# Three loads and one store change places in the DMA order of SyncE, in a fused attention and feed-forward kernel

## The reference

```python
xn = _layernorm(x, axis=-1)
# attention: 16 heads of 16 features
qkv = xn @ w_qkv.T + b_qkv
att = einsum('bhqd,bhkd->bhqk', q, k) / sqrt(16) + bias      # bias depends on (i - j) and the head
att = softmax(where(causal, att, -inf))
attn = einsum('bhqk,bhkd->bhqd', att, v) -> [B, T, C] @ w_proj.T + b_proj
# feed-forward: x and kernel rounded to float8 (e4m3), multiplied in float32, scaled back
return x + attn + ffn
```

## Time and profile before

| what | value |
|---|---|
| time, median of 3 runs | 825.46 us (824.64 to 831.89) |
| time of the profiled execution | 820.26 us |
| its span on the core | 818.5 us |
| granted TensorE clock, mean | 0.973 of full speed |
| PE busy | 747.2 us (91%) |
| DVE busy | 628.9 us (77%) |
| ACT busy | 581.0 us (71%) |
| POOL busy | 528.2 us (65%) |
| queue q1 | 102.96 MB, 60.4% of 16 engines |

### The profile page before, as it was taken

How to read it: one execution, slowest core, us unless ns; L and a number is a source line. 1 busy time by engine, 2 the same in 40 slices (tenths; PEclk the granted TensorE clock), 3 DMA queues, 4 the chain that set the end, 5 groups by cost and what they waited for, 6 DMA issues and landing times.

```text
span 818.5 us, 23154 instructions
## 1 busy us (share of the span) xinstructions
PE 747.2 (91%) x6313; PEld 510.0 (62%) x6313; DVE 628.9 (77%) x2395; ACT 581.0 (71%) x1258; POOL 528.2 (65%) x525
## 2 busy tenths in 40 slices
PE   6869999999999999999999999999999999999883
PEld 3546666666676667657676666657666666767552
DVE  3767878887977878788788878787787879778722
ACT  4236767777786877778687777778677777867671
POOL 6433568567666867667676757766685776667580
PEclk8859999999999999999999999999999999999998
DMA  6834666567566656666566657756665775666502
GB/s 170 165 68 95 114 145 123 129 148 144 127 138 153 118 130 138 138 145 137 141 121 151 123 127 162 142 126 137 148 117 123 155 143 124 139 130 121 120 24 86
DMA packets 55548, 106.07 MB, mean 130 GB/s; under 512 B 10464, under 2 KB 30432, under 8 KB 55520
## 3 DMA queue, kind: packets, MB, share of 16 engines
q1 hardware_dynamic: 53192, 102.96, 60.4%
q10 hardware_dynamic: 2328, 2.77, 1.0%
HBM read 18.68 MB, written 8.91 MB: 34 GB/s over the span
## 4 chain that ended last, share of the span: by engine, by line
PE 49%; ACT 15%; SPq 11%; issue 9%; DMA 7%; DVE 5%; ACTq 3%; DVEq 1%; POOL 0%; POOLq 0%
SPq L328 11%; PE misc_a L539 8%; PE misc_a L655 8%; PE scoreT_b L629 6%; PE misc_b L539 6%; ACT probs L911 6%; PE scoreT_a L629 3%; DMA stacks<-neg_max_T 3%; PE misc_b L655 3%; PE score_a L606 3%; PE score_c L606 2%; ACT qk_parts L818 2%; ACT out_T L884 2%; ACT attn_hi L893 2%; ACT xnT_hi L807 1%
## 5 line engine op out<-in xcount | busy, mean ns | idle before, releaser
L1187 POOL TENSOR_SCALAR_AFFINE_SELECT probs<-probs 128x512 f32<-128x512 f32 x256 | 159.5, 635 | 244.7 <-ACT probs L911 242.8
L989 DVE CUSTOM_DVE_ANT_0 score_b<-score_b,causal_mask_q 128x384 f32<-128x384 f32 (+3 forms) x321 | 161.9, 521 | 119.6 <-PE score_b L606 118.4
L989 DVE CUSTOM_DVE_ANT_0 score_a<-score_a,causal_mask_q 128x512 f32<-128x512 f32 x319 | 173.1, 559 | 8.1 <-PE score_a L606 4.1
L911 ACT ACTIVATE probs<-scoreT_b 128x384 f32<-128x384 f32 (+1 forms) x256 | 134.5, 525 | 60.7 <-issue 23.7
L989 DVE CUSTOM_DVE_ANT_0 score_c<-score_c,causal_mask_q 128x256 f32<-128x256 f32 (+3 forms) x384 | 171.4, 474 | 2.3 <-PE score_c L606 2.2
L911 ACT ACTIVATE probs<-scoreT_a 128x512 f32<-128x512 f32 (+1 forms) x256 | 145.6, 569 | 14.0 <-PE scoreT_a L632 7.4
L989 DVE DVE_READ_ACCUMULATOR2_ANT row_max<- 128x1 f32 x1024 | 142.9, 140 | 0.0
L911 ACT ACTIVATE probs<-scoreT_c 128x384 f32<-128x384 f32 (+1 forms) x256 | 136.2, 532 | 3.7 <-PE scoreT_c L632 3.3
L655 PE MATMUL misc_a<-probs,v_ones 128*32 128x128 f32 (+3 forms) x1536 | 131.2, 438 | 0.4 <-POOL probs L1187 0.4
L629 PE MATMUL scoreT_a<-stacks 64*128 64x512 f32 (+3 forms) x320 | 108.3, 358 | 21.8 <-DMA stacks<-neg_max_T 13.8
L629 PE MATMUL scoreT_b<-stacks 64*128 64x384 f32 (+3 forms) x320 | 119.5, 393 | 7.6 <-ACT probs L911 7.1
(11 more groups left out here) (241 smaller groups left out, 1948.9 us busy)
## 6 DMA issues: line engine op xcount, KB each, us to landing
stacks<-qk_parts SPq DMA_DIRECT2D x128, 512.0 KB, 8.1
x_ring<-in_L_attn_x SPq DMA_DIRECT2D x16, 512.0 KB, 3.6
xn<-recips SPq DMA_DIRECT2D x31, 256.0 KB
out<-x_ring SPq DMA_DIRECT2D x15, 512.0 KB, 3.0
attn<-out_T SPq DMA_DIRECT2D x48, 128.0 KB, 2.6
stacks<-neg_max_T SPq DMA_DIRECT2D x128, 4.0 KB
attn<-out_T ACTq DMA_DIRECT2D x16, 128.0 KB, 2.9
low_features<-neg_max_T SPq DMA_DIRECT2D x124, 4.0 KB
```

The lines of the kernel that those rows point to most:

```text
L911: A(probs_slot(g, k), STB[(SLOTS * g + k) % 3][:, 0:w], ACT.Exp).then_inc(exp_done, 1)
L989: last = V.tensor_tensor_reduce(bank, bank, CMQ[:, T - w:T], 1.0, LEAST, ALU.add, ALU.max, MX[:, g % 2, 8 * h + 4 + qt:8 * h + 5 + qt])
L1187: last = GP.affine_select(out=d, in_=d, compare_op=ALU.is_ge, fill=0.0, base=0, pattern=[[0, HU], [1, P]], channel_multiplier=-1)
```

## The change

SyncE's list of one batch is reordered. Before, the inverses' store came first, then x's load, the spread, and the next batch's first stack. Now x's load comes first, then the store, the stack, and the spread. No instruction of another engine moves, and nothing is added or taken away.

```diff
@@ -462,20 +462,20 @@
                     sp.wait_ge(st_ready, ROW * b)
                 load_stack(b, 3)
                 load_max(b, 1)
-                if not first:
-                    store_recips(b - 1)
                 if load:
                     if not first:
                         sp.wait_ge(out_stored, 16 * b)
                     sp.wait_ge(x_loaded, 16 * (b + 2))
                     load_x(b + 2)
                 if not first:
-                    spread_recips(b - 1, last)
+                    store_recips(b - 1)
 
                 if not last:
                     wait_alone(sp, (w_loaded, 16), (st_ready, ROW * b + SLOTS),
                                (ql_ready, 4 * (b + 1) + 2))
                     load_stack(b + 1, 0)
+                if not first:
+                    spread_recips(b - 1, last)
                 load_max(b, 2)
                 regroup(b, 0, first)
```

## The result

| kernel | median | runs | mean clock of the profiled run |
|---|---|---|---|
| before | 827.25 us | 4 (824.64 to 831.89) | 0.973 |
| changed | 875.64 us | 4 (871.65 to 886.7) | 0.933 |

The medians are of all four runs; the ratio, 1.056 with a 95% interval of 1.049 to 1.064, leaves out the run of 886.7 us, which fell into the slower of two states that executions of one kernel show. The forecast was 815 us, in a range of 811 to 828; it failed in sign and in size. The span of the profiled execution went from 818.5 to 872.5 us, 54 us more.

What follows compares the result with a forecast made beforehand. PE was taken as bound by its waits for the maxima, 13.8 us in all; 0.8 us off each gave 10.4 us, `divide`'s delay counted as nothing. Off the 825.46 us median that made 815 us, range 811 to 828.

Steps and rivals of the forecast that it cites:

- What bounds the kernel: PE is busy 91%; its largest wait is for the row maxima at unit (2,0), 13.8 us in 15 waits.
- A batch gets shorter by nearly what this wait loses: PE at (2,0): batch length less the wait for the maxima is constant within 0.4 us.
- x's load forward: SyncE: x's load issued once the second maxima are out, near 439 in batch 8; its 0.42 us issue costs nothing.
- The stack's earlier start: SyncE: the stack starts at 444.72 in place of 445.89 in batch 8, 1.17 us earlier.
- The spread moves behind the stack. Its issues end near 447.6, ...: SyncE, batch 8: the spread's issues end near 447.6, so the maxima are issued at most 0.3 us later.
- whole weight: DMA engines: the spread's full transfer time, estimated at 1.6 us, added between the stack and the maxima.
- best: Maxima in batch 8: the spread behind the stack costs nothing, their issue ends at 452.47 in place of 454.26, 1.8 us earlier.
- worst of this kind: Maxima in batch 8: the spread adds 1.6 us, their issue ends at 454.07, 0.2 us earlier.
- `divide`'s delay: POOL, batch 8: the spread lands at 454.3, so `divide` is 1.0 us late, costed at nothing.
- The slack of 1.5 us: POOL, batch 8: `divide` may start as late as 454.78 instead of 453.30 for nothing.
- The one on the slow side: POOL and DVE: a late spread makes `divide` the bound, 6 to 12 us slower, about 834; chance 0.15.
- The first rival: SyncE's DMAs: same bytes ahead of the maxima, 0.2 us a batch left, 822 us, no tellable change; chance 0.30.

Runs made afterwards that it cites:

- e5: Kernel before with a wait added on SyncE, so the third maxima are issued near 454.5 of batch 8 in place of 447.5; 886.01 us, ratio 1.076.
- e8: Kernel before with x's load ahead of the inverses' store and DVE's inversion one unit earlier, (0,7) for (0,8); 817.31 us, ratio 0.991.
- e9: Changed kernel with PE running ten extra products before its wait for the maxima of group 2, in batches 1 to 14; 853.23 us, ratio 1.038.
- e1: Kernel before with only x's load moved ahead of the inverses' store, the spread still ahead of the stack; 820.45 us, ratio 0.993.
- e2: Kernel before with only stack and spread exchanged, store and x's load in their old order; 871.94 us, ratio 1.057.
- e3: Changed kernel with the third maxima sent ahead of the spread; 906.86 us, ratio 1.100.
- e6: Kernel before with a wait added on POOL, so `divide` starts only after the exponential of unit (2,0); 866.46 us, ratio 1.050.
- e7: Kernel before with x's load moved directly behind the stack; 980.21 us, ratio 1.186.
- e10: Changed kernel with the spread between the two DMAs of the stack; 855.74 us, ratio 1.034.

## Why the prediction was wrong, step by step

- **What bounds the kernel** was right. The maxima at (2,0) are PE's largest single wait, e5 lengthened it and the kernel with it, e8 took most of it away and won time.
- **"A batch gets shorter by nearly what this wait loses"** rested on seven batches of one trace and was too good. In e8 the waits lost 11.3 us and the time 6.4. With the 10.4 us of waits that I forecast, the gain would have been about 6, an estimate from e8. In the other direction it breaks too, since the clock falls after the longer waits: of the change's 3.81 us a batch 1.96 are wait and 1.85 clock (e9).
- **x's load forward** was right: issued 0.6 us after the second maxima, 3.3 us ahead of the store, no cost (e1), 0.7% gain.
- **The stack's earlier start** was right: 467.15, against the end of DVE's L977 at about 467.1.
- **The step that failed: "The spread moves behind the stack. Its issues end near 447.6, ..."**, and the bound built on it, that the spread adds at most its "whole weight", 1.6 us, to the time from the stack to the maxima. I carried over the 1.34 us that these two issues took ahead of the stack. Behind it they took 6.28 us in the changed kernel, and 3.94 in e2. The 8.37 us became 10.55, outside my "best" and "worst of this kind", which both assumed that SyncE would issue maxima meanwhile. I also took the last maxima's 1.69 us to land as fixed; they take 2.92 behind the spread. Together the way from the stack's first issue to the landing of the maxima grew by 3.14 us on the mean, and against e3, which has no spread between the two, it is 3.95 longer. For the hold of the issue the trace had a row. In the setup of the kernel before, six stack DMAs are issued in a row; the timeline there shows the first two, and the third:

```profile
22.15 1.25 SPq L448 DMA_DIRECT2D stacks<-qk_parts  x2
23.44 3.87 SPq L365 DMA_DIRECT2D stacks<-qk_parts  x1
```

  The third is let through 27.31 - 22.15 = 5.16 us after the first. The spread's first DMA in the changed kernel: 472.37 - 467.15 = 5.22. I had seen that small maxima are held behind a stack, and took the hold for theirs, not for that of whatever stands third.
- **`divide`'s delay** was forecast at 1.0 us and was 3.56, by the same hold. That it cost next to nothing (7.1 us of DVE's waits in all) was luck: PE was late too. The slack of 1.5 us was right: in batch 8 of e6 POOL waits 3.42 us before `divide` and DVE 1.96 behind it, 1.46 less. The price behind it was missing: in e6 a wait of POOL of 3.6 us on the mean, before `divide`, cost 2.76 us a batch. The third mask, to which I had given over 2 us of room, comes late with it, and PE waits for it at L655, 12.9 us in all.
- **The rivals.** The one on the slow side named the hold of the spread's issue in its last sentences, but as a road to a late `divide`, at 834 us, and had 0.15. The hold's own path, through the maxima that stand behind the spread in the same list, was missing, though the text said what the wait of SyncE held. The first rival counted bytes ahead of the maxima and had them land 0.2 us earlier; they landed 1.95 later. The Trainium skill's page "DMA: Bandwidth & Descriptors", section "Queues, rings and completion order", was cited for it. Its ring order is not refuted: the maxima's longer landing behind the spread (2.88 and 3.66 us against 1.72) agrees with it. But it says nothing of when SyncE can put the maxima into the queue. Why the spread adds over 3 us there and not 1.6 stays open.

## What to carry to other kernels

A DMA's issue has no price of its own: read it at the place to which it moves, behind what will be in flight there, and look for that pair in the setup or in the tail if the loop does not have it. If an issue can be held, the next thing to ask is what small and urgent work stands behind it in the same list; here 4 KB DMAs paid for a 256 KB one, while they waited to be issued and again on their way. And when a change makes two things late, removing one can leave the other or make it worse, as e3 did: of the orders tried here, only those with the spread in front of the stack were not slower. Sending the maxima by another engine's list was not tried.

## What the runs showed of the hardware

| where | held DMA | let through, after the first stack DMA's issue |
|---|---|---|
| before, setup | third stack DMA, 512 KB | 5.16 us |
| changed | spread's first DMA, 256 KB from DRAM | 5.22 us |
| e7 | x, 512 KB from DRAM | 5.25 us |
| e10 (one stack DMA ahead) | spread's second DMA | 5.08 us |

What is held does not matter in these four, nor where it reads from: the third large DMA, counted from a stack DMA, waits in SyncE until about 5.2 us after that one was issued. In the old order, with the spread first and the stack behind it, none of the four is held in batches 2 to 14; in batch 1 the stack's second DMA takes 2.33 us to issue, so the order is not all that matters. e2, where x's load goes just ahead of the stack, does not fit this simple count, and the maxima, 8 pieces each, are let in earlier (3.7 and 6.3 us for the first two in batch 8). What resource it is stays open. The Trainium skill, "Perfetto Trace Analysis", section "DMA Instruction — HWDGE (DVE, Sync)", has the profiler's time of an issue end only after all descriptors are generated, and knows a descriptor buffer that can be too small for them; the long issues here fit that, but no run here measured the buffer.

TensorE's clock fell from 2.4 to 1.2 GHz after waits of about 3 us (2.94 in the batch shown), and in the kernel before not after those of up to 1.6 us. In between there is no clean border: in the changed kernel it fell after a wait of 1.68 us and not after one of 1.76, and in e10 after 1.41 and not after 1.43. Ten products that compute nothing, run during the wait, kept it up (e9).
